# Attention in a one-core hybrid kernel: features cut into pieces of 512 columns, maxima split after the turn and sent from SP, five buffers in the first part

## The reference, cut to what matters

```python
q, k, v = split(x @ Wq), split(x @ Wk), split(x @ Wv)          # 16 heads of 8 channels
scores_dot = einsum('bihd,bjhd->bhij', q, k) * scale
def _amp_norm(t):
    a = softplus(t)
    return a / sqrt(mean(a * a, axis=-1, keepdims=True) + AMP_EPS)
q_phi, k_phi = pi * tanh(split(x @ Wqp)), pi * tanh(split(x @ Wkp))
q_cos, q_sin = q_amp * cos(q_phi), q_amp * sin(q_phi)          # the same for k
scores_phase = (q_cos . k_cos + q_sin . k_sin) * scale
scores = scores_dot + lam * scores_phase
scores = where(causal, scores, -inf); attn = softmax(scores)
out = (attn @ v) @ Wo;  x = x + out
```

## Time and profile before

| | us |
|---|---|
| median of three runs | 1336.99 |
| the three runs | 1331.23, 1336.99, 1340.11 |
| the profiled execution | 1336.39 |
| its span, first to last instruction | 1334.6 |
| PE busy | 1106.7 (83%) |
| DVE busy | 868.8 (65%) |
| ACT busy | 573.2 (43%) |
| PE granted clock, mean | 0.899 of full |

### The profile page before, as it was taken

The page is one execution under the profiler, slowest core; times in us unless marked ns, Lnnn a source line. Parts: engine busy times, 40 slices in busy tenths (PEclk is TensorE's granted clock), DMA queues, the critical chain, the costliest instruction groups (busy, mean ns, idle before and its releaser), DMA issues. The chain is left out here.

```text
span 1334.6 us, 15092 instructions
## 1 busy us (share of the span) xinstructions
PE 1106.7 (83%) x4960; PEld 626.4 (47%) x4960; DVE 868.8 (65%) x1823; ACT 573.2 (43%) x964; POOL 265.8 (20%) x294
## 2 busy tenths in 40 slices
PE   4777777764899999758578988989889958999997
PEld 1222222221666666424355655656556635666664
DVE  3799989874656554556476677667686725665543
ACT  1233333321433433257355656557565543333332
POOL 1444444441000000140021121211212220000000
PEclk9899888775899999888678989889899998999998
DMA  4000000000141222008977776867757311322311
GB/s 186 0 1 1 0 0 0 0 0 0 64 128 64 96 96 64 1 0 255 289 226 203 167 184 166 217 171 157 188 123 155 74 60 68 116 76 82 110 64 64
DMA packets 43769, 130.61 MB, mean 98 GB/s; under 512 B 5552, under 2 KB 7600, under 8 KB 36784
## 3 DMA queue, kind: packets, MB, share of 16 engines
q1 hardware_dynamic: 42608, 129.17, 34.7%
q10 hardware_dynamic: 1088, 0.52, 0.2%
HBM read 90.62 MB, written 38.54 MB: 97 GB/s over the span
## 5 line engine op out<-in xcount | busy, mean ns | idle before, releaser
L1707 ACT ACTIVATE moe_hidden<-moe_ps_h 128x512 f32<-128x512 f32 x256 | 138.6, 594 | 209.5 <-PE moe_ps_y L1642 209.4
L1381 DVE TENSOR_REDUCE attn_maxima<-attn_ps_p 128x1 f32<-128x512 f32 (+3 forms) x235 | 145.2, 636 | 79.4 <-PE attn_ps_p L945 74.7
L1803 DVE TENSOR_TENSOR moe_gated<-moe_ps_y,moe_gate_all 128x512 f32<-128x512 f32 x112 | 77.4, 691 | 165.3 <-issue 83.0
L1309 POOL TENSOR_SCALAR_AFFINE_SELECT attn_probs<-attn_probs 128x512 f32<-128x512 f32 x128 | 81.7, 675 | 324.6 <-ACT attn_probs L1178 324.6
L1631 PE MATMUL moe_ps_h<-moe_x_high,moe_w_high 128*128 128x512 f32 x256 | 137.2, 536 | 4.6 <-DVE moe_w_low L1824 2.9
L940 PE MATMUL attn_ps_p<-attn_stack 96*128 96x384 f32 (+3 forms) x341 | 121.8, 399 | 22.5 <-DVE attn_maxima L1381 21.6
L1642 PE MATMUL moe_ps_y<-moe_hidden,experts_in_w 128*128 128x512 f32 x256 | 119.9, 592 | 0.0
L1642 PE MATMUL moe_ps_y<-moe_hidden,experts_again_w 128*128 128x512 f32 x256 | 119.9, 592 | 0.0
L987 PE MATMUL attn_ps_q<-attn_stack 128*128 128x128 f32 (+3 forms) x343 | 109.7, 384 | 6.7 <-DMA attn_stack<-attn_neg_max 6.4
L564 POOL TENSOR_TENSOR rwkv_rs<-rwkv_recept,rwkv_state 128x512 f32<-128x512 f32 x64 | 75.9, 1187 | 146.3 <-DVE rwkv_state L655 141.6
L1632 PE MATMUL moe_ps_h<-moe_x_low,moe_w_high 128*128 128x512 f32 x256 | 102.4, 400 | 0.0
(11 more groups left out here) (233 smaller groups left out, 2034.1 us busy)
## 6 DMA issues: line engine op xcount, KB each, us to landing
moe_gate_all<-moe_gates SPq DMA_DIRECT2D x128, 256.0 KB, 5.0
attn_kept<-attn_parts SPq DMA_DIRECT2D x16, 1536.0 KB, 6.4
attn_stack<-attn_kept SPq DMA_DIRECT2D x64, 384.0 KB
attn_stack<-attn_kept SPq DMA_DIRECT2D x64, 192.0 KB
attn_value<-attn_values SPq DMA_DIRECT2D x6, 1792.0 KB, 9.9
attn_values<-attn_probs SPq DMA_DIRECT2D x4, 1792.0 KB, 22.4
attn_values<-attn_v_ones SPq DMA_DIRECT2D x2, 1792.0 KB, 21.1
experts_in_w<-in_w SPq DMA_DIRECT2D x2, 1024.0 KB, 10.8
```

The costliest lines, as they stand in the source:

```text
L1309: nc.gpsimd.affine_select(out=tile, in_=tile, compare_op=ALU.is_ge, fill=0.0, base=0, pattern=[[0, 4], [1, P]], channel_multiplier=-1).the ...
L1381: nc.vector.tensor_reduce(maxima[:, u % 2, h:h + heads, t], tiles, AX_X, ALU.max).then_inc(g_free, 1)
L1707: fn(hidden[:, s, k * T:(k + 1) * T], ps_h[s][k][:], ACT.Gelu).then_inc(gelu_done, 1)
L1803: tt(out, ps_y[g % 2][:], gate_all[:, b % 2, e, :], ALU.mult).then_inc(gated_ready, 1)
```

## The change

- **First part.** The batches are taken in the order `FIRST` = 0, 3, 4, 1, 5, 6, 7, 2. Five early buffers instead of three: two more lie in the space of the stack tiles of q = 1. Batches 3 to 7 each have an early buffer of their own; batch 2 comes last and goes into `value[0]`, once batch 0's `low` is done, and is neither stored nor fetched. `turn(1)` is moved ahead of `phases(0)`, and the norm's `scale` and `statistics` run one turn further ahead. Batch 0's amplitudes are made after turn 3 (was 1), its high and low parts in turns 4 and 5 (were 2 and 3), and PE takes the two means before turn 4's queries and keys (before: after turn 2's values).
- **Features in pieces.** Every operation on 1024 or 1536 columns becomes two or three on 512 columns, each with a semaphore of its side, and they are spread over slots 4 to 39 (before 10 to 36).
- **Maxima.** PE turns the plain maxima (128x16), ACT copies minus the result as the high part (16x128), and DVE makes the low part from PSUM (one operation on 16x128 at slots 4, 14, 24, 34); the two small DVE operations on 128x16 are gone. SP starts the transfers, two for each send (`send_maxima`), instead of one from ACT.
- **Slots of the loop.** Output turns go from slot 8 to 9 (of q's first ten), `normalise` from 8 to 10 and 28 to 30, the output's turn and projection from 14, 16 to 16, 18, the addition from 16 to 19, the means from 18, 20 to 20, 26.

```diff
+    FIRST = [0, 3, 4, 1, 5, 6, 7, 2]
         def home(b):
-            return value[b] if b < 2 else early[(b - 2) % 3]
+            return value[b % 2] if b < 3 else early[b - 3]
+            def send_maxima(u, half):
+                sp.wait_ge(neg_low, 2 * u + half + 1)
+                for part in range(2):
+                    sp.dma_start(stack[0][u % 2][ROWS + part:ROWS + part + 1, 4 * half:4 * half + 4, :].bitcast(F32),
+                                 neg_max[half][:, part, :].bitcast(F32)).then_inc(neg_max_landed[half], 16)
-            store(2)
+            store(3)
+            store(4)
             keep(0, 0)
             keep(0, 1)
-            store(3)
+            store(5)
...
+            store(7)
+            send_maxima(0, 0)
+            for s in range(2):
+                keep(1, s)
             for b in range(NB):
+                send_maxima(2 * b, 1)
                 if b < LAST:
                     refill(b, 0, 0)
+                send_maxima(2 * b + 1, 0)
                 if b + 3 < NB:
                     fetch(b + 3)
                 if b < LAST:
                     refill(b, 0, 1)
+                send_maxima(2 * b + 1, 1)
+                if b < LAST:
                     refill(b, 1, 0)
+                    send_maxima(2 * b + 2, 0)
                 if b + 2 < NB:
                     keep(b + 2, 0)
                     keep(b + 2, 1)
...
 (PE)            def turn_maxima(name, b, u):
-                pe.wait_ge(split_ready, 2 * u + half + 1)
+                pe.wait_ge(g_free, u * TILES + 11 * half + 11)
 (ACT)           def take_maxima(name, b, u):
-                fn(neg_max[half][:], ps_f[0:8 * TC, 0:P], ACT.Copy).then_inc(f_free, 1)
-                act.wait_ge(f_free, TURN[name, b] + 1)
-                act.dma_start(stack[0][u % 2][ROWS:ROWS + 2, 4 * half:4 * half + 4, :].bitcast(F32),
+                fn(neg_max[half][:, 0, :], ps_f[0:4 * TC, 0:P], ACT.Copy, scale=-1.0).then_inc(neg_high, 1)
 (DVE)
+            def split_maxima(name, b, u):
+                v.wait_ge(neg_high, 2 * u + half + 1)
+                stt(neg_max[half][:, 1, :], ps_f[0:4 * TC, 0:P], -1.0, neg_max[half][:, 0, :].bitcast(F32), ALU.mult,
+                    ALU.subtract).then_inc(neg_low, 1)
+                v.wait_ge(neg_low, 2 * u + half + 1)
+                v.sem_inc(f_free, 1)
 (DVE)           def features(b, k):
-                if k == 32:
-                    low(b, 0)
-                if k == 36:
-                    low(b, 1)
...
+                if k == 37:
+                    low(b, 1, 1)
+                if k == 39:
+                    low(b, 1, 2)
```

More of the change, by code:

```diff
@@ L743, in attention_stage @@
         norm = Norm(nc, sb, sem, x, minus_half, started)
-        stack = [[sb(f"stack{s}{q}", [P, UH, T], F32R) for q in range(2)] for s in range(2)]
+        with ExitStack() as before_stacks:
+            early = [before_stacks.enter_context(nc.sbuf_tensor(f"attn_early{s}", [P, UH, T], F32)) for s in range(2)]
+        late = [sb(f"stack{s}1", [P, UH, T], F32R) for s in range(2)]
+        stack = [[sb(f"stack{s}0", [P, UH, T], F32R), late[s]] for s in range(2)]
         value = [sb(f"value{s}", [P, 7, T]) for s in range(2)]
@@ L1241, in between @@
                     features(b + 2, 20 * q + k)
-                if b == 0 and q == 0 and k == 2:
-                    high(1, 0)
-                if b == 0 and q == 0 and k == 4:
-                    high(1, 1)
+                if b == 0 and q == 0 and k in (0, 1):
+                    for part in range(3):
+                        high(1, k, part)
             loads.wait(act)
             nc.scalar.preload_act_table_set("silu_and_others")
-            fn(col[:, 1:2], col[:, 0:1], ACT.Tanh).then_inc(lambda_ready, 1)
@@ L1439, in between @@
                     features(b + 2, 20 * q + k)
-                if b == 0 and q == 0 and k == 3:
-                    low(1, 0)
-                if b == 0 and q == 0 and k == 5:
-                    low(1, 1)
+                if b == 0 and q == 0 and k in (2, 3):
+                    for part in range(3):
+                        low(1, k - 2, part)
             norm.statistics(v, 0)
             loads.wait(v)
-            v.wait_ge(lambda_ready, 1)
+            v.wait_ge(prepared, LAMBDA_READY)
             nc.vector.memset(col[:, ONE], 1.0)
@@ L1473, in _ @@
[L1473 to L1477 removed]
+            nc.vector.tensor_copy(ident_b[:], ident[:]).then_inc(prepared, 1)
+            for n in range(NB):
+                if n + 2 < NB:
+                    norm.scale(v, n + 2, (turned, n + 2), FIRST[n + 2])
+                if n + 3 < NB:
+                    norm.statistics(v, n + 3, FIRST[n + 3])
+                take_queries(n)
+                take_values(n)
+                if n == 3:
+                    v.wait_ge(prepared, COLUMNS_READY)
+                    for s in range(2):
+                        softplus(0, s)
+                    for s in range(2):
+                        amplitude(0, s)
+                        scale_circle(0, s, 1)
+                        scale_circle(0, s, 2)
+                if n in (4, 5):
+                    for part in range(3):
+                        low(0, n - 4, part)
@@ L1478, in _ @@
+            take(0, range(8))
+            for s in range(2):
+                softplus(1, s)
+            take(0, range(8, 14))
+            split_maxima("M0a", 0, 0)
+            for s in range(2):
+                amplitude(1, s)
+            take(0, range(14, 18))
+            for s in range(2):
+                scale_circle(1, s, 1)
+                scale_circle(1, s, 2)
             take(0, range(18, TILES))
-            scale_circle(1, 1)
             for b in range(NB):
```

528 lines of the change are left out of this document (281 added, 247 removed).

## The result

The changed kernel takes 1358.94 us (median of four runs, 1357.30 to 1359.89), the kernel before 1338.55 us beside it (four runs, 1331.23 to 1349.47). The ratio of the mean times is 1.0144 with a 95% interval of 1.0073 to 1.0216. The forecast was 1330 us, with a range up to 1352: wrong in sign and outside its range. The profiled execution spans 1357.6 us, 23.0 more than that of before.

What follows compares the result with a forecast made beforehand. PE was taken to set the end, losing time in waits and clock. First part -7.9, batches 1 to 5 -2.5, batch 6 +5.8, batch 0 -2.1: -6.7 us against 1336.4 gives 1330 us, range 1290 to 1352.

Steps and rivals of the forecast that it cites:

- The first part: Before the loop: fewer stores ahead give 13.2 us, a later second keep costs 5.3; loop starts 7.9 us sooner.
- The pieces: Feature operations in the loop: DVE's longest hold falls from 1.75 to 0.7 us, DVE's total stays.
- The last low: Piece at slot 39: second keep issued 2.1 us after the batch's start, where it was 1.0 before it.
- From the second keep to M0b, 13.9 us: Distance from second keep's issue to PE's use of M0b, putting slot 10 at 16.0 us, a new 5.7 us wait.
- M0b later still: Rival: both keep go out back to back, slot 10 at 21 us, 1362 us in all; chance 0.13.
- The queue of the sends, charged nothing: Moving the maxima's sends from ACT to SP costs 0, since the separate queue did not overtake before.
- The clock: Slots behind the wait at slot 10 run at the lower clock level, costing 2.7 us; bounds 0 and 3.7.
- Slots 10 to 39: This stretch of a batch takes 35.1 us: 32.57 plus 1.0 for two means plus 1.5 left over.
- Batch 0: First batch of the loop: slot 10 at about 18.2 us, 56.0 us against 58.16, so -2.1.
- my case: The forecast's own main case, a total of -6.7 us, chance 0.48, alone 1316 to 1344 us.
- No wait at slot 10: Rival: M0b lands by 10.6 us, 1273 us in all; chance 0.28 together with a shorter-wait case of 1300 us.
- DVE still binds: Rival: what remains in slots 10 to 39 is 5 us, not 1.5, in six batches: 1351 us; chance 0.11.

Runs made afterwards that it cites:

- The hold: Changed kernel with SP issuing the refill of query half 0, half 0, only once M0b has landed: 1349.8 us (1.0090).
- the version with pieces: Changed kernel with each keep sent as three 512 KB pieces, each once its low is done, and side 1's second half three slots earlier: 1317.1 us (0.9851).
- neither cure alone: Changed kernel with either side 1's second half three slots earlier (1356.2 us, 1.0123) or the first keep ahead of M0a's send (1356.2 us, 1.0158).
- the two together: Changed kernel with the first keep ahead of M0a's send and side 1's second half three slots earlier: 1332.4 us (0.9968).

## Why the prediction was wrong, step by step

**The store's wait** went, as said: no store appears among ACT's or DVE's waits of the first part.

**The first part**, forecast -7.9, came to -3.3 us. Both terms were off. By the rows below, the second `keep` was issued by 616.48 + 4.93 = 621.4, before by 605.97 + 8.48 = 614.5: 7.0 later, not 5.3. From there to the loop it took 46.9 us for 57.2, 10.2 less and not 13.2. The loop still starts behind a transfer of the maxima (timelines, before and after):

```profile
605.97 8.48 SPq L828 DMA_DIRECT2D attn_kept<-attn_parts  x2
```

```profile
616.48 4.93 SPq L835 DMA_DIRECT2D attn_kept<-attn_parts  x2
...
668.34 0.77 PE L1007 MATMUL attn_ps_q<-attn_stack 128*128 128x512 f32 x1 [1.97 <-DMA attn_stack<-attn_neg_max]
```

**The pieces**: right. DVE's long hold is gone, PE's longest wait for a reduction in batches 1 to 6 falls from 1.6 to 0.6 us, and slots 30 to 39 take 10.7 us for 15.3.

**The last low**: right in kind. The second `keep` was to go out 2.1 us into the batch (1.33 + 0.68 make 2.0); it does at 2.9. The piece starts 1.7 us into the batch instead of 1.33, and takes 1.15 us there in every batch instead of 0.68; why it is slower in this place no run shows.

**From the second keep to M0b, 13.9 us**: the term that was mis-sized, 16.2 us on average. I moved a distance read in one execution to a new time without asking what else is issued meanwhile. The hold shows the larger part, 1.7 us: a refill that the faster slots 0 to 9 bring forward to 10.4 us. I had forecast those slots at full clock and did not ask what they trigger. Of the other 0.6 us, 0.2 are the difference between the one execution of batch 6 (13.9) and the mean of batches 1 to 6 (14.1); what the rest is stays open. With the `keep` 0.8 us later than said, slot 10 starts at 19.1 instead of 16.0, 5 x 3.1, some 15.6 us, in batches 1 to 5 and 3.0 in batch 6.

**The rival "M0b later still"** had 0.13. Its test, slot 10 later than 17.1 us, is met, and its 1362 us is near the result, but its mechanism is only half there. SP does hold the first `keep` behind M0a's send, to 1.7 us before the batch where I argued 5, because DVE's split stands behind the reductions; yet the second follows 4.4 us later, so the first is nearly drained and costs the changed kernel little. It matters as a second lock: with the second `keep` alone moved forward, slot 10 still came at 18.3 us.

**The queue of the sends, charged nothing**: right. With the `keep` in the same places slot 10 came at 17.0 us with the sends on ACT's queue and at 17.4 with them on SP's. The Trainium skill's "DMA: Bandwidth & Descriptors", section "Queues, rings and completion order", says that each DMA engine goes round the queues it has work for, packet by packet. That M0b on its own queue would then land soon after its issue was my inference, and the traces are against it: not in the kernel before (issued at 953.52 in batch 5, its first packet on ACT's queue runs at 958.9, its last at 960.0), nor in the changed one with the sends moved back, nor in the old one with both `keep` late. What moving the sends did cost is another thing: on SP they are links in an in-order chain, and a send that waits for DVE holds the `keep` behind it. That order I left unpriced.

**The clock**, 2.7 us charged behind the wait: a little high. Slots 10 to 19 at 0.78 take 13.96 us, at 1.00 in the version with pieces 12.19, and the same slots in batches 1 and 5 of it 11.6: 1.8 to 2.3.

**Slots 10 to 39** without the clock were to take 35.1 us. With it, 37.8; they took 39.5, 8 us in five batches. The term is the means, 1.0 us. (The forecast's -0.5 a batch is -0.6 by its own sum, 53.8 against 54.4.) Slots 20 to 29 of batches 1 to 5 take 14.4 us at a clock of 1.00, those of batch 6 10.3. In these 4.1 us are two means of 1.10 us each, in full and not half, and three waits for `ps_f` around them (timeline after, batch 3):

```profile
877.53 1.10 PE L940 MATMUL attn_ps_f<-attn_soft,attention_in_mean_head 128*128 128x512 f32 x2 [0.96 <-DVE x_rows L1467]
880.22 0.27 PE L994 MATMUL attn_ps_f<-identity,attn_maxima 128*16 128x128 f32 x1 [0.29 <-ACT attn_soft L1177]
889.51 0.63 PE L1042 MATMUL attn_ps_f<-identity,attn_o_rows 128*128 128x128 f32 x4 [0.57 <-ACT attn_soft L1177]
```

2.2 + 1.8 = 4.0, as the stretches have it: PE is busy 12.5 us of these slots in batch 4 and 10.3 in batch 6, and idle 1.9 and 0. What ends these waits is DVE's sum of the output and ACT's logarithm, which the change moved; that the split stands behind their lateness is argued, not shown. The prediction had one sentence on ACT's and DVE's new hand-over inside `ps_f` and priced it at 0.

**Batch 0** was forecast -2.1 and came to -2.1, with slot 10 at 18.3 us for 18.2: there both `keep` were known to stand ahead of M0b, and the sum counted them.

Together: 4.6 us of the miss in the first part, 24 in batches 1 to 5, 2 in batch 6, 30.6 against a miss of 29.7 in all; the difference is rounding and the rest of the span. The largest part is the stall: slot 10 at 19.1 us and not at 16.0 is 18.6 of them, 2.3 us a batch in the way from the second `keep` to M0b and 0.8 in the `keep` itself. (The "1316 to 1344" of my case does not follow from the bounds it names: they give 1309 to 1341.) "No wait at slot 10" was wrong at any size: 51 of the 53 us of waits stand there. "DVE still binds" was wrong too, though the time missing in slots 20 to 29 looked like it.

## What to carry to other kernels

A distance between two transfers read from a trace holds only for the backlog that stood ahead of both; before moving it, list everything in flight at the new time and what the in-order queue lets out when. A send that waits for a late result should not stand in front of a large transfer that is ready, and a large transfer whose parts become ready over time goes out in those parts, into stretches where the DMA engines have room. Two causes that lie one behind the other need a run that removes both: here neither cure alone could be told from none, and the two together gave 27 us.

## What the runs showed of the hardware

A transfer of 8 KB lands 1.8 to 2.5 us after its issue when nothing is left ahead of it (M0b in the run with both `keep` behind it), and 9.9 to 11.4 us behind two `keep` and a refill (the changed kernel, batches 1 to 6). A queue of its own did not take it past them: in batch 4 9.2 and 10.4 us on ACT's queue, 10.5 and 10.9 on SP's.

More surprising is the hold. A refill issued 2.7 us behind M0b (911.05 against 908.39), on the same queue, delayed M0b while it was still on its way: 8.9 us from issue to landing without it, 10.5 with it, on average over batches 1 to 6. The same shows in M0b's packets where it has ACT's queue: in the kernel before, with the refill issued after them, its 34 packets pass within 0.5 to 1.1 us of one another in batches 1 to 5; with both `keep` held back, and the refill issued at 916.15, they run from 916.4 to 920.5. So a transfer here was slowed by what followed it too, not only by what stood ahead.
